# A two-layer decoder on one core: pair sums, a moved output projection and single maxima matmuls in two self attentions

## What is computed

```python
q, k, v = heads(x @ q_w.T + q_b), heads(x @ k_w.T + k_b), heads(x @ v_w.T + v_b)
q, k = apply_rope(q), apply_rope(k)            # layer 0 alone
probs = softmax(einsum('bhqd,bhkd->bhqk', q, k) * scaling)
out = einsum('bhqk,bhkd->bhqd', probs, v).reshape(B, S, D) @ out_w.T + out_b
```

## Time and profile before

| | us |
|---|---|
| median of three runs | 1841.78 |
| the profiled execution | 1841.2 |
| its span, first to last instruction | 1839.2 |
| TensorE matmul busy | 1554.5 (85%) |
| VectorE busy | 1125.8 (61%) |
| ScalarE busy | 879.6 (48%) |
| GpSimd busy | 473.6 (26%) |
| mean granted TensorE clock | 0.946 of full speed |

### The profile page before, as it was taken

The page is one execution under the profiler, slowest core; times in us unless marked ns, Lnnn a source line. Parts: engine busy times, 40 slices in busy tenths (PEclk is TensorE's granted clock), DMA queues, the critical chain, the costliest instruction groups (busy, mean ns, idle before and its releaser), DMA issues.

```text
span 1839.2 us, 27993 instructions
## 1 busy us (share of the span) xinstructions
PE 1554.5 (85%) x9286; PEld 602.0 (33%) x9287; DVE 1125.8 (61%) x1676; ACT 879.6 (48%) x1056; POOL 473.6 (26%) x415
## 2 busy tenths in 40 slices
PE   1898999998949983688689999999979999999938
PEld 1323323233216661334332323333222333323213
DVE  4664756656644555899556464646545676767675
ACT  1353362443523332788646454454645455564734
POOL 0523415115130004422241212213133131414120
PEclk9999999999979996799989999999989999999969
DMA  3710201103032446200030110202222020203002
GB/s 103 258 28 23 69 0 52 40 2 89 0 125 98 142 139 130 48 1 1 1 107 21 25 45 0 69 0 69 91 75 63 24 68 23 68 0 91 0 29 92
DMA packets 80848, 106.15 MB, mean 58 GB/s; under 512 B 14112, under 2 KB 51360, under 8 KB 80672
## 3 DMA queue, kind: packets, MB, share of 16 engines
q1 hardware_dynamic: 77216, 97.14, 17.8%
q0 software_dynamic: 3584, 8.39, 2.2%
HBM read 49.26 MB, written 18.35 MB: 37 GB/s over the span
## 4 chain that ended last, share of the span: by engine, by line
PE 55%; issue 13%; DVE 10%; ACT 7%; POOL 2%; SPq 1%; DMA 1%; POOLq 1%; DVEq 0%; ACTq 0%
PE ps L416 26%; PE ps L735 14%; PE ps L824 6%; PE ps L683 3%; ACT arena L931 2%; PE ps L707 1%; DVE arena L1143 1%; SPq L642 1%; PE ps L1912 1%; DVE xn L188 1%; PE ps L1591 1%; DVE arena L1745 1%; PE ps L756 1%; POOLq L147 1%; ACT arena L1640 1%
## 5 line engine op out<-in xcount | busy, mean ns | idle before, releaser
L931 ACT ACTIVATE arena<-ps 128x1024 f32<-128x1024 f32 x384 | 372.0, 1024 | 174.0 <-PE ps L824 173.5
L735 PE MATMUL ps<-arena 128*32 128x512 f32 x3072 | 389.3, 612 | 33.2 <-DVE arena L1012 24.5
L975 DVE TENSOR_REDUCE arena<-ps 128x2 f32<-128x1024 f32 x256 | 306.3, 1220 | 152.1 <-PE ps L683 151.9
L416 PE MATMUL ps<-xt,w 128*128 128x512 f16 (+1 forms) x1872 | 297.6, 311 | 21.4 <-DVEq L147 9.7
L824 PE MATMUL ps<-arena 97*128 97x512 f16 (+1 forms) x768 | 208.9, 384 | 8.7 <-ACT arena L931 6.0
L416 PEld LDWEIGHTS ps<-xt,w 128*128 128x128 f16 (+1 forms) x1872 | 154.3, 100 | 158.6 <-issue 50.8
L416 PE MATMUL ps<-w,arena 128*128 128x512 f16 (+1 forms) x804 | 178.7, 379 | 12.6 <-issue 12.6
L1255 POOL TENSOR_TENSOR arena<-arena 128x512 f16<-128x512 f32 x96 | 115.8, 1209 | 224.0 <-ACT arena L917 188.7
L913 ACT ACTIVATE arena<-ps,arena 128x512 f32<-128x512 f32 x96 | 65.7, 686 | 208.0 <-PE ps L416 170.3
L1143 DVE TENSOR_SCALAR arena<-arena 128x1024 f32<-128x1024 f32 x128 | 106.6, 838 | 65.9 <-ACT arena L931 65.1
L735 PEld LDWEIGHTS ps<-arena 128*32 128x32 f32 x3072 | 76.9, 110 | 208.0 <-issue 180.0
(11 more groups left out here) (195 smaller groups left out, 1854.9 us busy)
## 6 DMA issues: line engine op xcount, KB each, us to landing
arena<-arena SPq DMA_DIRECT2D x576, 64.0 KB, 2.0
raw<-in_ctxT SPq DMA_DIRECT2D x8, 1024.0 KB, 5.4
raw<-in_ffn_parts SPq DMA_DIRECT2D x16, 512.0 KB, 3.5
sorted_x<-arena SPq DMA_DIRECT2D x1, 4864.0 KB, 25.7
arena<-sorted_x SPq DMA_DIRECT2D x19, 256.0 KB, 3.5
sorted_y<-arena SPq DMA_DIRECT2D x19, 256.0 KB, 2.1
out<-x SPq DMA_DIRECT2D x16, 256.0 KB, 2.0
x<-in_x SPq DMA_DIRECT2D x1, 3072.0 KB, 14.3
```

The lines of the kernel that those rows point to most:

```text
L416: last = pe.matmul(out, left[l](cl[k]), right[r](cr[k]), start=start and k == 0 and a == 0, stop=stop and k == n - 1 and a == 2)
L735: last = pe.matmul(self.m.ps[HD * j:HD * (j + 1), 7 if ones else 6, :], left, self.pt[:, u % 2, j * S:(j + 1) * S], start=kb == 0, stop=kb ...
L931: act.activation(self.pt[:, u % 2, 2 * h * S:(2 * h + 2) * S], flat(self.m.ps[:, 2 * h:2 * h + 2, :]), ACT.Exp, scale=SOFTMAX_SCALE).then_ ...
L975: v.tensor_reduce(self.mx[:, g % 2, j:j + 2, t:t + 1].rearrange("p h t -> p (h t)"), self.slot_banks(item, b), AX.X, ALU.max).then_inc(sel ...
```

## The change

In both self attentions:

1. **Pair sums.** VectorE adds the exponentials of two key tiles (`dve_add`, in two halves of 128x1024 f32), and TensorE multiplies that sum by ones (`pe_pair_sum`): 8 such groups in a batch for 16. They stand at the end of units 3, 5, 7, 9, 11, 13 and 15, and the eighth after the first Q/K chunk of the next batch. The exponentials get a third buffer and the pair sum a place of its own, both in the memory of the Q/K chunks `qf`.
2. **Order of a batch.** The output of batch b-1 comes between Q/K and V of batch b. Only the last batch's output stands alone behind the loop. The first batch is written out by itself, with plans of its own.
3. **Maxima.** `in_halves` splits the 12 matmuls of a chunk or tile; the tables now have two steps for each, in the middle and at the end. Nearly all pairs go there, mostly one at a time.
4. **Contexts.** Two banks in turn (6 and 5). VectorE multiplies the context straight from its bank; ScalarE's copy and GpSimd's multiplication go. The reading of the sums and the multiplication are one unit apart.
5. **Output.** For all but the last batch ScalarE copies it from its bank and GpSimd adds it to `x`.
6. **Rope.** GpSimd multiplies by the sines ahead of the rotation matmul; VectorE has one operation for two in a rotation. The final norm and scatter of batch b-1 lie in the heads and projections of batch b.
7. **Stores of maxima** all come after the 48 stacking DMAs.

In all three attentions an `x` is one token tile (4 transposes, 128x512), four for two. Some semaphores are renamed so that phases share them.

```diff
+def in_halves(pe, out, left, right, between, start=True):
+    half = C // 2
+    three_passes(pe, out, left, right, range(half), range(half), start, False)
+    between()
+    return three_passes(pe, out, left, right, range(half, C), range(half, C), False, True)
...
+            self.pts = [self.pt[:, 0], self.pt[:, 1], chunks[:, 0:HG * S]]
+            self.pair_sum = chunks[:, HG * S:2 * HG * S]
...
-    WITH_PROJ = ('', '', 'pp', 'pp', 'pp', 'p', 'pp', 'pp')
-    WITH_V = ('pp', 'mpp', 'pp', 'mpp')
-    WITH_UNIT = {1: ',p,,p', 2: ',p,,p', 3: ',,p,', 4: 'p,,,p', 5: ',p,,', 6: 'm,p,,p', 7: ',,p,', 8: ',,p,', 9: ',p,,', 11: 'm,,,', 13: ',,,x', 15: ',,,x'}
-    ROPE_WITH_PROJ = ('', '', '', '', 'pp', 'pp', 'pp', 'pp')
-    ROPE_WITH_V = ('pp', 'pp', 'mpp', 'pp')
-    ROPE_WITH_UNIT = {0: ',,p,', 1: ',m,p,', 2: 'p,,,pp', 3: ',,p,', 4: ',p,,p', 5: ',,p,', 6: 'm,p,,p', 7: ',,p,', 8: ',p,,p', 9: ',,p,', 10: ',p,,m', 13: ',,,x', 15: ',,,x'}
...
+    WITH_PROJ = ("", "", "p,p", "p,p", "p,p", "p,p", "p,mp", "p,p")
+    WITH_OUT = ("p,p", "p,p", "p,mpp", "p,p")
+    WITH_V = ("p,p", "p,pp", "p,mp", "p,pp")
+    WITH_UNIT = {0: ",p,,", 3: "m,,,", 8: ",,,x", 10: ",,,x", 12: ",,,x", 14: ",,,x"}
+    FIRST_PROJ = ("", "", ",pp", ",pp", "p,pp", "p,pp", "m,pp", ",pp")
+    FIRST_V = ("p,pp", "p,pp", "p,mpp", "p,pp")
+    FIRST_UNIT = {0: "m,pp,,pppp", 3: "m,,,", 8: ",,,x", 10: ",,,x", 12: ",,,x", 14: ",,,x"}
+    ROPE_WITH_PROJ = ("", "", "", "p,p", "p,p", "p,p", "p,p", "p,mp")
+    ROPE_WITH_OUT = ("p,pp", "p,p", "p,pp", "p,mp")
+    ROPE_WITH_V = ("p,pp", "p,p", "mp,pp", "p,p")
+    ROPE_WITH_UNIT = {0: ",p,,p", 3: "m,,,", 8: ",,,x", 10: ",,,x", 12: ",,,x", 14: ",,,x"}
+    ROPE_FIRST_PROJ = ("", "", "", ",pp", ",pp", ",pp", "p,pp", "p,pp")
+    ROPE_FIRST_V = ("pp,pp", "pp,pp", "p,mpp", "mp,pp")
+    ROPE_FIRST_UNIT = {0: "m,pp,,pppp", 3: "m,,,", 8: ",,,x", 10: ",,,x", 12: ",,,x", 14: ",,,x"}
...
+        for half in range(2):
+            order = ((0, self.kst, (0, 0, 1)), (1, self.qst, (0, 1, 0)))
+            for n, (w, stack, parts) in enumerate(reversed(order) if self.cross else order):
+                sp.wait_ge(*self.at(self.fl, b * self.NPROJ + 4 * half + (2 * (n + 1) if self.cross else n + 3)))
+                for r, part in enumerate(parts):
+                    for j in range(HG):
+                        sp.dma_start(stack[HD * r:HD * (r + 1)].rearrange("p (c j) t -> p c j t", j=HG)[:, 2 * half:2 * half + 2, j, :],
+                                     self.qf[HD * j:HD * (j + 1), w, part, 2 * half:2 * half + 2]).then_inc(self.stacked[half], 16)
+        if not self.cross:
+            for g in range(C):
+                self.sp_maxima(sp, g, b)
...
+    def pe_turn_x(self, pe, i, b):
+        m = self.m
+        item = ("x", i)
+        if b is not None:
+            self.slot_wait(pe, self.slot_free, item, b, 0)
+            pe.wait_ge(*self.at(self.norm.xn_ready, b * T + i + 1))
+        elif i >= 2:
+            self.slot_wait(pe, self.slot_free, ("x", i - 2), b, 1)
+        for c in range(C):
+            last = pe.transpose(self.bank_x(i, b)[:, c * P:(c + 1) * P], m.xn[:, i, c * P:(c + 1) * P], m.ident[:])
...
+    def context(self, g):
+        return self.m.ps[:, 6 if self.cross or g % 2 == 0 else 5, :]
+    def p(self, u):
...
+        elif u < NH and u % T == T - 1:
+            self.pe_pair_sum(pe, u // 2 - 1, b)
+        elif T < u < NH and u % T == 1:
+            self.pe_pair_sum(pe, (u - T) // 2 + 1, b)
+    def pe_pair_sum(self, pe, n, b):
+        if n % 2 == 0 and n:
+            pe.wait_ge(*self.at(self.sums_read, b * C + n // 2))
+        pe.wait_ge(*self.at(self.paired, 2 * (b * self.ADDS + n + 1)))
+        self.pe_sum(pe, self.pair_sum, n % 2 == 0, n % 2 == 1).then_inc(self.pair_read, 1)
...
+        for n in range(self.NPROJ):
+            self.pe_proj(pe, n, b)
+            if n == 0 and not first:
+                self.pe_pair_sum(pe, self.ADDS - 1, b - 1)
+            if self.rope and n:
+                self.pe_rotate(pe, n - 1, b)
+            self.pe_planned(pe, b, "proj", n, 1)
+        if self.rope:
+            self.pe_rotate(pe, self.NPROJ - 1, b)
+        if not first:
+            self.weights.wait(pe, 3)
+            pe.wait_ge(*self.at(self.cl, b * C))
+            for i in range(T):
+                self.wait_free(pe, ("v", i), b)
+                self.pe_out(pe, i, [0, 1])
+                self.pe_planned(pe, b, "out", i, 0)
+                self.pe_out(pe, i, [2, 3]).then_inc(self.out_full, 1)
+                self.pe_planned(pe, b, "out", i, 1)
+        self.pe_project_values(pe, b)
+        self.pe_heads(pe, b)
...
+    def act_out(self, act, i, b):
+        act.wait_ge(*self.at(self.out_full, b * T + i + 1))
+        if i >= 2:
+            act.wait_ge(*self.at(self.out_added, b * T + i - 1))
+        else:
+            act.wait_ge(*self.at(self.t1_ready if self.rope else self.fl, (b + 2) * self.NPROJ))
+        act.activation(self.qb[:, i % 2, :], self.bank(("out", i)), ACT.Copy, scale=1.0 / WSCALE).then_inc(self.out_free, 1)
+    def act_wait_block(self, act, u, h, b):
+        before = u - 3
+        if u == 2:
+            for half in range(2):
+                act.wait_ge(*self.at(self.stacked[half], (b + 1) * 24 * 16))
+        if before >= 0:
+            act.wait_ge(*self.at(self.values_done, b * NH + before + 1))
+            act.wait_ge(*self.at(self.paired, 2 * (b * self.ADDS + before // 2) + h + 1))
...
+    def dve_multiply(self, v, g, b):
+        self.dve_reciprocals(v, g, b)
+        v.wait_ge(*self.at(self.cl, b * C + g))
+        v.wait_ge(*self.at(self.inverted, b * C + g + 1))
+        v.tensor_tensor(self.ctxn, self.context(g), self.sums, ALU.mult).then_inc(self.normed, 1)
...
+        if not first:
+            self.dve_context(v, C - 1, b - 1)
+        for n in range(self.NPROJ):
+            if self.rope and n:
+                self.dve_rotate(v, n - 1, b)
+            if n == 4 and not first:
+                self.dve_last_low(v, b - 1)
+            for step in range(2):
+                self.dve_planned(v, b, "proj", n, step)
+        if self.rope:
+            self.dve_rotate(v, self.NPROJ - 1, b)
+        if not first:
+            for i in range(T):
+                for step in range(2):
+                    self.dve_planned(v, b, "out", i, step)
+        for i in range(T):
+            for step in range(2):
+                self.dve_planned(v, b, "v", i, step)
+        self.dve_self_heads(v, b)
...
+    def dve_add(self, v, n, b):
+        if n == 0:
+            for half in range(2):
+                v.wait_ge(*self.at(self.stacked[half], (b + 1) * 24 * 16))
+        v.wait_ge(*self.at(self.pair_read, b * self.ADDS + n))
+        for h in range(2):
+            cols = slice(2 * h * S, (2 * h + 2) * S)
+            v.wait_ge(*self.at(self.exp_done[h], b * NH + 2 * n + 2))
+            v.tensor_tensor(self.pair_sum[:, cols], self.p(2 * n)[:, cols], self.p(2 * n + 1)[:, cols], ALU.add).then_inc(self.paired, 1)
...
+            self.dve_planned(v, b, u - 1, 3)
+            for step in range(3):
+                self.dve_planned(v, b, u, step)
+            if g and kb == 1:
+                self.dve_read_sums(v, g - 1, b)
+            if u % 2:
+                self.dve_add(v, u // 2, b)
+            if g and kb == 2:
+                self.dve_multiply(v, g - 1, b)
+            if u == (3 if self.rope else 0):
+                if self.rope:
+                    v.wait_ge(*m.x_all)
+                self.norm.dve_stats(v, own, (0, 1))
+            if u == (4 if self.rope else 0):
+                self.norm.dve_stats(v, own, (2, 3))
+                self.norm.dve_aggregate(v, b)
+            if self.rope and not first:
+                if u == 0:
+                    self.dve_final_moments(v, b - 1)
+                if u == 2:
+                    self.dve_final_apply(v, b - 1)
+            for i in range(T):
+                if u == (6, 6, 8, 8)[i] if self.rope else u == (4, 4, 6, 6)[i]:
+                    self.norm.dve_apply(v, b, own, lambda i: m.xn[:, i, :], [i])
...
-        v.tensor_tensor(self.bank(item), self.bank(item), self.sin, ALU.mult).then_inc(self.sin_part, 1)
-        v.wait_ge(*self.at(self.sin_part, b * self.NPROJ + n + 1))
...
+                g.tensor_tensor(self.qs[:, n % 2, :], self.qb[:, n % 2, :], self.sin, ALU.mult).then_inc(self.qs_ready, 1)
                 g.tensor_tensor(self.t1[:, n % 2, :], self.qb[:, n % 2, :], self.cos, ALU.mult).then_inc(self.t1_ready, 1)
...
+            for i in range(T):
+                xs = slot(m.x, (b - 1) * T + i)
+                g.wait_ge(*self.at(self.out_free, (b - 1) * T + i + 1))
+                g.tensor_tensor(xs, xs, self.qb[:, i % 2, :], ALU.add).then_inc(self.out_added, 1)
```

597 lines of the change are left out of this document (342 added, 255 removed).

## The result

The changed kernel takes 1829.28 us (median of five runs, 1828.70 to 1831.72) against 1840.26 of the kernel before (five runs beside them): ratio 0.9943, 95% interval 0.9929 to 0.9958. The forecast was 1828.0, faster. Its profiled execution spans 1827.1 us, for 1839.2 before.

The account below looks back on a forecast made before the run. TensorE's instruction stream was taken as the bound. Second self attention -12.0, rope -8, first batches +2.0 and last batches +4.6 sum to -13.4 us: 1828 against the profiled 1841.2, range 1793 to 1857.

Parts of the forecast that it names:

- Second self attention: Three later batches: projections 56.9 plus heads 42.9 make 99.8 us for 103.8, so -12.0 us in all.
- the third rival: Projections give it all back: a single mid-chunk pair costs 0.55 us, not 0.43; 17 us, 1843, no change; chance 0.12.
- Rope's Q/K: Rope's later batches: TensorE waits 4.9 us for VectorE's reductions at middle pairs and an m, making Q/K 38.4 us.
- Rope's heads: Rope's later batches: 47.3 us with the eighth sum, including 2.5 following additions, 1.5 GpSimd meetings and 1.5 ScalarE.
- The clock: Rope's later batches: half of the slower stretch's 1.7 us is counted, 0.9 us a batch, as waits change place.
- between -8 and +1.7: The -8: rope's three later batches forecast at 116.7 us each for 119.35, so -2.7 x 3.
- The meetings with GpSimd: Heads: an addition that meets a GpSimd operation costs VectorE 0.84 us more; 1.5 us a batch in rope.
- the rival's half of 16: VectorE becomes the heads' bound: half of 16 additions meet GpSimd at 0.84 us each, +31, so 1859; chance 0.18.
- First and last batches: Self attentions: first batches +1.5 (rope) and +0.5, each between -4 and +6; last batches +2.3 twice.
- the bound of 6: Sign of being wrong: a first batch of a self attention costs over 6 us.
- Cross attention: Only finer turns: 0.3 us more of TensorE, VectorE reads sums about 1 us earlier; nothing, within 3.
- the prediction's own signs of being wrong: A self attention's batch not 2 to 5 us shorter, additions over 1.3 us, or first batches costing over 6 us.

Follow-up runs that it names:

- the kernel with both edits: Changed kernel with rope's final norm statistics moved to unit 1 and GpSimd's bias additions moved into the V stretch in later batches: 1808.79 us, ratio 0.9832 to before.
- the second execution: The changed kernel run once more without an edit: 1830.99 us, median of six runs; the profiled one took 1834.0.

## Why the prediction was right in its total, and where not

*Second self attention, -12.0 for -12.2.* Right by each step: 0.43 for a group, 0.96 and half the f32 matmuls for a unit, VectorE 36.2 of 42.0 us in the heads, heads 42.0 and projections 57.7 for 42.0 and 57.8 (the eighth sum counted with the projections). Additions took 1.22 but for three in sixteen, which took 2.2. The experiment with pairs side by side confirms the price and shows what the third rival feared, at 0.43 already: the singles give back 17 us. (That rival's own sum is off: 1828 and 17 make 1845, and only three of the four batches have the 18 groups, so 13 us and 1841.) No experiment undoes the pair sums, the contexts or the place of the output one by one; what they bring is read from the rows alone. The Trainium skill's rule on changing the tiling mode ("TensorEngine Tiling (Array Packing)", Key Properties) agrees with this: a group of two costs 0.43 us as a group of one does.

*Rope's Q/K, 4.9 us of waits forecast, 4.4 measured*: 0.35 three times and 1.23 at pairs, 2.07 at the m. The step stands.

*Rope's heads, 46.4 without the eighth sum for 50.5.* The forecast had 5.5 us of waits in them (2.5 for following the additions, 1.5 for meetings, 1.5 for ScalarE), and 6.4 came. That is near in size by luck, since I hadn't placed VectorE's operations in order: there the final norm's statistics stand ahead of a reduction on which TensorE's first values wait, 3.25 us in each batch. That the kernel before had a wait near the same spot, 1.28 us, was in my rows. The other 3.2 us are TensorE's busy time, 44.1 for 40.9, mostly the clock.

*The clock: the step that failed.* I counted half of the low clock seen before, 0.9 us a batch or 2.7 in three, because "the waits change their place". Against the kernel with both edits, whose three batches run at full clock, TensorE is busy 10.1 us more in the three. The wait ahead of the first values was longer than the old one and the low clock came at it in every batch, and behind the m's wait in two of three. Of the 9.7 us between -8 and +1.7, 7.4 are this term; 1.2 come from the first of the three batches, which took 118.1 us before and not 119.35; the rest is waits and sizes.

*The meetings with GpSimd.* The price was 0.84, it measured (4.45 - 2.35) / 2 = 1.05 each; the number, 27 of 128 or three to four a batch, was far below the rival's half of 16. The mean of all additions is 1.42 us against the median of 1.22, so 128 x 0.20 / 8 = 3.2 us of VectorE a batch. The forecast had looked for meetings at the bias additions in rope; 23 of the 27 are with the low halves of the contexts, in both self attentions. VectorE was not the bound of the heads, but the bias additions out of them were worth 11 us; that they stood where VectorE was late already is my reading of it. The Trainium skill's rule on shared SBUF interfaces ("GPSIMD Engine Reference", Specifications) agrees with these rows; that section gives no time for it.

*First and last batches.* Last: +1.4 and +1.9 for +2.3, right. First: +5.0 for +1.5 in rope, within the bound of 6; +2.0 for +0.5 in the other. In rope the Q/K stretch took 10.4 us more (49.5 for 39.1) and not 5. Of it 2.4 is an earlier start that the first rotation waits away (it starts at 56.12 for 55.83, both behind work of others); the rest is waits of pairs and m's on reductions and a clock of 0.86 for 0.91. V took 5.0 more for some 3. The heads ran at a clock of 0.89 and 0.86 from first to last score, behind the waits of unit 0, which I hadn't priced:

```profile
111.00:156.20 45.20, 42.30 (x254) 11.22 (x253) 37.66 (x49) 32.35 (x37) 4.39 (x4) 0.89 0.00 1
982.10:1029.80 47.70, 42.32 (x252) 11.25 (x253) 37.18 (x48) 33.41 (x37) 4.40 (x4) 0.86 0.01 1
```

*Cross attention, 0 within 3 for -12.2.* I saw that VectorE would read the sums about 1 us earlier (0.87 measured), and put that at nothing. I cited the row of 3.54 us without seeing in it that sixteen matmuls take 1.92 at full clock: 1.6 us a batch that hang on that wait. Four times 0.87 + 1.62 is 10.0 of the 12.2; the rest is the clock of its first Q/K stretch.

So 1828 was right by luck, by two errors of opposite sign: rope came 12 us longer than forecast (8.1 for -4.2), cross attention 12 shorter; in the second execution the errors are 10 and 5. Only the second self attention was forecast for the right reasons. Two of the prediction's own signs of being wrong came true: the rope batch isn't 2 to 5 us shorter (356.8 us in three before, 358.6 and 355.3 after), and additions last over 1.3 us in the mean.

What stays open: why the same wait is followed by the low clock in one batch and not in the next; and the 10.2 and 13.7 us of low clock in the first heads of both self attentions, of which, in the second, an edit took away the wait of 3.42 us and 3.4 us of low clock.

## What to carry to other kernels

Where an engine gets new work, write its operations down in order and find, for each, who waits for the one behind it; a sum that fits in the stretch (36 of 42 us) says nothing of a single wait of 3 us. Price a wait of TensorE with the clock that follows it, by comparing the rows right behind it with the same instructions elsewhere. And pack what forces a change of tiling into as few groups as the other engine can follow.

## What the runs showed of the hardware

- A wait of 1.7 us is followed by eight f32 matmuls at 1.07 us in one batch and at 1.94 in another of the same execution. The 2.07 us wait of rope's first m, in the third batch, is followed in the changed kernel by the low clock, in the one with earlier bias additions not:

```profile
313.85 0.28 PE L756 MATMUL ps<-ident,arena 128*16 128x128 f32 x1 [2.07 <-DVE arena L1160]
...
314.38 1.94 PE L850 MATMUL ps<-arena 128*128 128x512 f32 x2
```

```profile
311.38 0.28 PE L756 MATMUL ps<-ident,arena 128*16 128x128 f32 x1 [2.07 <-DVE arena L1160]
...
311.91 1.12 PE L850 MATMUL ps<-arena 128*128 128x512 f32 x2
```

 Both have the same instructions there, with the same waits of 0.35 ahead of them. So the length of one wait doesn't decide it.
- A gain of 3 us in one phase was lost by the clock, 2 us of it in the next phase (27.4 for 25.4 us with the same instructions). Two profiles of one kernel differ by 5 us in span (1827.1 and 1832.2): TensorE is busy 3.0 us longer with the same 8774 instructions, and idle 2.1 longer. Differences of single phases under some 5 us are to be read from rows at full clock.
- An addition of 128x1024 f32 from two SBUF inputs takes 1.17 to 1.23 us in 101 of 128 cases, and 2.17 to 2.30 in 27, all beside an operation of GpSimd with two SBUF inputs of 128x512. Here the first of two additions takes 2.19 us beside such a subtraction and the second 1.2:

```profile
1210.87 1.19 POOL L1414 TENSOR_TENSOR arena<-arena 128x512 f16<-128x512 f32 x1 [11.18 <-ACT arena L1037]
...
1210.96 3.32 DVE L1321 TENSOR_TENSOR arena<-arena 128x1024 f32<-128x1024 f32 x2
```

 Not every overlap costs VectorE: 16 additions that overlap such a subtraction for some 0.9 us still take 1.21 to 1.23. GpSimd's bias additions take 1.6 to 1.7 us each in the heads, as means of four, and 1.26 in the V stretch, where VectorE only reduces from PSUM.
